# One transposing transfer of a group's split context where there were two

## What is computed

```python
x = _layernorm(x + _L0_attn_ref(x, ...))          # linear attention
x = _layernorm(x + _L0_xattn_ref(x, ctx, ctx, ...))
x = _layernorm(x + _L0_ffn_ref(x, ...))
# inside _L0_xattn_ref:
    attn = jax.nn.softmax(scores, axis=-1)
    ctx = jnp.einsum('bhqk,bhkd->bhqd', attn, V)
    ctx = ctx.transpose(0, 2, 1, 3).reshape(B, S, D)
    out = jnp.einsum('bsd,ed->bse', ctx, Wo) + bo
```

## Time and profile before

| | |
|---|---|
| median of 3 runs | 673.92 us (671.83 to 674.71) |
| profiled execution | 673.73 us, of which the span of the trace is 671.9 us |
| busy, share of the span | PE 96%, PEld 68%, DVE 79%, ACT 66%, POOL 67% |
| mean granted TensorE clock | 0.992 of full speed |
| transfers `cT<-cs` | 30, median 3.4 us from issue to landing |

### The profile page before, as it was taken

The page is one execution under the profiler, slowest core; times in us unless marked ns, Lnnn a source line. Parts: engine busy times, 40 slices in busy tenths (PEclk is TensorE's granted clock), DMA queues, the critical chain, the costliest instruction groups (busy, mean ns, idle before and its releaser), DMA issues.

```text
span 671.9 us, 30473 instructions
## 1 busy us (share of the span) xinstructions
PE 646.1 (96%) x13160; PEld 456.5 (68%) x13160; DVE 532.7 (79%) x1479; ACT 440.6 (66%) x761; POOL 450.5 (67%) x497
## 2 busy tenths in 40 slices
PE   9999999999999999999999999999999999999695
PEld 6766767766766766676676667667677666776474
DVE  1656678788888878898787888878888888777687
ACT  4546465849578584957758494875849487886362
POOL 3234134867769596777959677695977779687552
PEclk9999999999999999999999999999999999999798
DMA  8102122362452434344453536236343634431400
GB/s 335 33 18 34 36 49 53 37 109 52 88 91 50 110 51 100 50 96 83 50 114 49 98 51 114 65 51 112 66 90 50 121 50 69 70 74 35 81 34 33
DMA packets 118905, 49.53 MB, mean 74 GB/s; under 512 B 109425, under 2 KB 109810, under 8 KB 118642
## 3 DMA queue, kind: packets, MB, share of 16 engines
q1 hardware_dynamic: 118770, 47.57, 36.6%
HBM read 16.88 MB, written 4.19 MB: 31 GB/s over the span
## 4 chain that ended last, share of the span: by engine, by line
PE 77%; POOL 9%; DMA 5%; issue 3%; DVE 3%; ACT 2%; SPq 1%; POOLq 0%; DVEq 0%; ACTq 0%
PE bank L330 14%; PE bank L347 8%; PE bank L320 7%; PE bank L400 4%; PE bank L428 4%; PE bank L443 4%; DMA cT<-cs 2%; POOL gall L1104 2%; PE bank L343 2%; PE bank L270 2%; PE bank L287 2%; PE bank L511 2%; PE bank L313 2%; PE bank L272 2%; PE bank L271 2%
## 5 line engine op out<-in xcount | busy, mean ns | idle before, releaser
L330 PEld LDWEIGHTS bank<-Mh,GT 128*32 128x32 f32 x4096 | 110.6, 110 | 25.9 <-issue 20.0
L330 PE MATMUL bank<-Mh,GT 128*32 128x128 f32 x4096 | 126.9, 274 | 1.4 <-issue 1.0
L897 DVE TENSOR_REDUCE mx<-bank 128x8 f32<-128x512 f32 x128 | 78.2, 682 | 13.8 <-PE bank L400 13.6
L1104 POOL TENSOR_TENSOR gall<-gall,lnr 128x512 f32<-128x512 f32 x56 | 71.1, 1281 | 16.8 <-DVE st L867 16.8
L846 DVE COPY GT<-bank 128x512 f32<-128x512 f32 x76 | 49.7, 687 | 35.4 <-PE bank L330 19.9
L662 ACT ACTIVATE PT<-bank 128x512 f32<-128x512 f32 x128 | 64.7, 621 | 10.7 <-PE bank L428 10.7
L1062 POOL TENSOR_TENSOR rstd<-ve,mhalf 128x4 f32<-128x4 f32 x64 | 66.5, 1039 | 5.3
L347 PE MATMUL bank<-Cb,qT 128*64 128x128 f32 x1024 | 66.8, 273 | 0.0
L320 PE MATMUL bank<-kp,xs 64*128 64x512 f32 x256 | 64.3, 617 | 0.0
L1109 POOL TENSOR_TENSOR gs<-gall,gs 128x512 f16<-128x512 f32 x56 | 64.0, 1162 | 0.1
L549 ACT ACTIVATE Mrow<-bank 64x128 f16<-64x128 f32 x16 | 4.3, 271 | 86.3 <-PE bank L409 86.3
(11 more groups left out here) (196 smaller groups left out, 1672.2 us busy)
## 6 DMA issues: line engine op xcount, KB each, us to landing
xT<-in_xT SPq DMA_DIRECT2D x16, 256.0 KB, 3.0
xs<-in_x_nat SPq DMA_DIRECT2D x16, 256.0 KB, 3.8
cxT<-in_cxT SPq DMA_DIRECT2D x16, 256.0 KB, 3.8
out_y<-yo SPq DMA_DIRECT2D x15, 256.0 KB, 2.0
Qm<-in_Wvp SPq DMA_DIRECT2D x1, 1024.0 KB, 7.2
gT<-gs SPq DMA_TRANSPOSE x56, 3.5
gall<-in_Wff SPq DMA_DIRECT2D x1, 768.0 KB, 9.9
small<-in_small SPq DMA_DIRECT2D x1, 523.0 KB, 8.4
```

What stands on the lines that cost most here:

```text
L330: m = e.matmul(bk[32 * j:32 * j + 32, tile(g_)], GT[b % 4][:, tile(hh, 32)], Mh[:, tile(hh)], start=True, stop=True)
L897: e.tensor_reduce(mx[s % 2][:, c0:c0 + 8], bank[uses["score", s, i][0]][:, :].rearrange("p (n k) -> p n k", k=64), AX.X, ALU.max).then_inc ...
L1104: e.tensor_tensor(g[t][:, :], g[t][:, :], lnr[:, :], ALU.mult).then_inc(s_gs, 1)
```

## The change

The two halves' tiles `cs[0]`, `cs[1]` and `cT[0]`, `cT[1]` become halves of one tile each, of 1024 columns. SP issues one transfer for both, at the place of the second one and after the second half's low part; the first half's issue is gone. One semaphore stands for the whole transfer, so `proj0` and `proj1` both wait for it, and so does ACT before it overwrites either half for the next group.

```diff
-        rs, cn, cT = [...], [...], [sb(f"cT{i}", 512, F16) for i in two]
-        cs = [sb(f"cs{i}", 512, F16) for i in two]
+        rs, cn, cT = [...], [...], sb("cT", 1024, F16)
+        cs2, cT2 = sb("cs", 1024, F16), cT
+        cs, cT = [cs2[:, 512 * i:512 * i + 512] for i in two], [cT2[:, 512 * i:512 * i + 512] for i in two]
...
                 else:
                     w.wait_ge(s_xwl, 1)
-                    w.wait_ge(s_cT[tp], 16 * (s + 1))
+                    w.wait_ge(s_cT, 16 * (s + 1))
...
-            def cturn(s, tp):
-                w.wait_ge(s_cl, 2 * s + tp + 1)
-                if s > 0:
-                    w.wait_ge(*filled("proj", s - 1, tp))
-                e.dma_start(cT[tp][:, :].rearrange("p (n c) -> p n c", n=4), cs[tp][:, :], transpose=True).then_inc(s_cT[tp], 16)
+            def cturn(s):
+                w.wait_ge(s_cl, 2 * s + 2)
+                if s > 0:
+                    w.wait_ge(*filled("proj", s - 1, 1))
+                e.dma_start(cT2[:, :].rearrange("p (n c) -> p n c", n=8), cs2[:, :], transpose=True).then_inc(s_cT, 16)
...
-                elif name == "cs":
-                    cturn(s, t)
+                elif name == "cs" and t == 1:
+                    cturn(s)
```

More of the change, by code:

```diff
@@ L147, in decoder_kernel @@
         mx, Mrow, M2 = [sb(f"mx{i}", 64) for i in two], [sb(f"Mrow{i}", 128, F16, 64) for i in two], [sb(f"M2{i}", 1024, F16) for i in two]
-        rs, cn, cT = [sb(f"rs{i}", 32) for i in two], [sb(f"cn{i}", 256) for i in two], [sb(f"cT{i}", 512, F16) for i in two]
-        cs = [sb(f"cs{i}", 512, F16) for i in two]
+        rs, cn, cT = [sb(f"rs{i}", 32) for i in two], [sb(f"cn{i}", 256) for i in two], sb("cT", 1024, F16)
+        cs2, cT2 = sb("cs", 1024, F16), cT
+        cs, cT = [cs2[:, 512 * i:512 * i + 512] for i in two], [cT2[:, 512 * i:512 * i + 512] for i in two]
         x2 = [sb(f"x2{i}", 512) for i in two]
@@ L154, in decoder_kernel @@
         gT = [gTs[:, 1024 * t:1024 * t + 1024] for t in range(4)]
-        gT32, cT32, tpw = [v.bitcast(F32) for v in gT], [v[:, :].bitcast(F32) for v in cT], xT
+        gT32, cT32, tpw = [v.bitcast(F32) for v in gT], [v.bitcast(F32) for v in cT], xT
         st, mv, ve, rstd = [{k: sb(n + k, c) for k in "1234"} for n, c in (("st", 24), ("mv", 8), ("ve", 4), ("rstd", 4))]
@@ L171, in decoder_kernel @@
         s_nr, s_ms, s_x2c = sem("mean_rstd"), sem("mean_part"), sem("x2_less_mean")
-        s_ch, s_cl, s_cT = sem("c_hi"), sem("c_lo"), [sem(f"c{t}_transposed") for t in two]
+        s_ch, s_cl, s_cT = sem("c_hi"), sem("c_lo"), sem("c_transposed")
         s_xwh, s_xwl = sem("xW_hi"), sem("xW_lo")
@@ L671, in chi @@
                 if s > 0:
-                    w.wait_ge(s_cT[tp], 16 * s)
+                    w.wait_ge(s_cT, 16 * s)
                 e.activation(cs[tp][:, 0:256], cn[tp][:, :], ACT.Copy).then_inc(s_ch, 1)
```

## The result

The changed kernel takes 677.3 us (median of 20 runs, 672.39 to 679.22) against 673.93 us for the kernel before (20 runs, 671.01 to 677.03): a ratio of 1.0051, with a 95% interval from 1.0031 to 1.0070, so 3.4 us more. Measured again, beside the last experiments and with runs of the kernel before beside it, it was 680.59 against 675.0 us, 1.0087 (1.0065 to 1.0109), 5.9 us more. I go by these ratios; they are not exactly the quotients of the two medians, and differ from them by up to 0.2%. Both intervals lie above no change. The forecast was 676.4 us.

What follows compares the result with a forecast made beforehand. PE, busy 96% of the span, was taken to set the pace outside the ends. From the profiled 673.73 us, 673.73 - 3.7 + 3.2 + 0.6 + 2.6 = 676.4 us, with an 8 in 10 range of 672.5 to 680.

Steps and rivals of the forecast that it cites:

- The removed waits: Periods, second projection of groups 2, 4 and 7: PE's waits between the two projections can't occur any more, -3.7 us.
- The late transfers in the periods: First projection of the 12 period groups: a bit under half the merged transfers delayed to about 4.2 us, +3.2 us.
- SP's queue: One issue of 1.2 us gone from each group, ahead of the `gT` issues: costed at nothing, bounds 0 and -2 us.
- Group 13: Tail, group 13's first projection: starts later because it waits for the whole transfer, +0.6 us, bounds 0 and 2.
- Group 14: Tail, group 14's first projection: the only transfer is issued at 631.20, PE goes on at 634.4, not 631.82, +2.6 us.
- The slow clock stays: Rival, tail: clock still 1.2 GHz at the last group's probabilities, 2 to 2.5 us more, 678.6 us; chance 0.12.
- Late as a rule: Rival: merged transfers take 4.2 to 4.7 us in most groups and in the tail, 681.8 us; chance 0.09.
- Never late: Rival, periods: the merged transfer is never late, so the 3.2 us go, 673.2 us; chance 0.18.
- hidden by the tail: Rival, tail: something else holds the last group's probabilities, so group 14 costs little, 673.8 us; chance 0.07.
- One fixed cost less per group: Rival: each transfer is paid in full, so dropping 15 gives 638 us; chance 0.02, shared with anything beyond 670.5.

Runs made afterwards that it cites:

- the shifted code: PE's code shifted by some 36 matmuls with smaller fillers at the start: changed kernel 683.2 us, 1.0124; kernel before 677.27 us, 1.0029, both against the kernel before.

## Why the prediction held

The time came out 0.9 us above the forecast and inside the range of 672.5 to 680. The second measurement, 680.59, lies just outside, beside a kernel before that was itself 1 us slower. The mechanism held term by term, with luck in two sizes.

**The removed waits, -3.7 us, held.** The waits between the two projections are gone in every group, and nothing else took their place there.

**The late transfers in the periods, +3.2 us, held in number, and in size with luck.** I took a bit under half of 12 as delayed to about 4.2 us. Six were, by 3.75 to 4.87, mean 4.25; two of these were still covered. The other four cost PE, as the distance between starts less the 0.20 us of an unhindered one, 0.77 + 1.18 + 0.46 + 0.82 = 3.2 us. The net of the two terms, -0.5 us, stands against -0.8 (-2.4 to +0.7) for the kernel that merges only there. By the working's own numbers a late transfer costs 4.2 - 3.1 less a spare of 0.6 to 0.8, that is 0.3 to 0.5 us and not the 0.6 that I put in, so the term should have read 1.6 to 2.7, and its upper bound 5 to 8 and not 12. The measured spare is 0.6 us in each of the four (4.45 - 3.1 - 0.77 in group 5); they were later than I had assumed, 4.5 us in mean, and that made up for it. What I had missed is why a transfer is late: I had it as a chance in each group, where, as far as the sorting shows, it is a packet of code that falls there. It recurs: groups 3, 5, 8, 10 and 12 were late in both profiles of the changed kernel, at 3.75 to 4.97 us.

**SP's queue at nothing: held.** The `gT` waits went from 1.0 to 0.9 us in sum.

**Group 13, +0.6 us, held where its transfer is on time**: 0.7 us in the second profile (1.22 against 0.52). In the first the transfer took 4.42 us and cost 2.2, just above the bound of 2 that I had set. The term left out that this transfer can be late like the others.

**Group 14, +2.6 us, held against the one profile of before**: from the scores to the projection 2.75 and 2.77 us more in the two profiles. PE's idle time there was 4.47 us, and 5.39 in the second, where I had 5.2; what decides is when PE can go on, 3.4 us after the issue, itself 3.1 us after the scores began, as before. The distance to the end stayed at 40 us, as the step said that it would: all of the shift went through. But I took the 631.82 of that profile as the kernel's own time, though the late first half stands in it. Against the 2.14 us seen where it was on time the merge costs 4.35 us here. How often it is late in the kernel before isn't known: it was in the kept trace and, at 4.4 us, in that of the shifted code.

**The tail is undersized by the runs.** The two terms make 3.2 us, the profiles 3.5 to 4.9, the kernel merged in the tail alone 5.0 (3.3 to 6.7). Part of the difference is group 13's late transfer, and part can be the first half of group 14 in the kernel before: where it is on time, the two terms make 5 to 6.5 us. The intervals do not decide between these.

**The rivals.** *The slow clock stays* is refuted by the row it named: the granted clock reads 1.00 from 638 to 641, and the distance to the end did not grow. In the second profile, where the low level holds for about 5 us behind the projection and not 3, it is 40.1 and not 39.8. The Trainium skill, page "TensorE: Matmul & The Clock Gate", section "HAM oscillation — how this bites in real kernels", has the penalty on top of the wait. Here the clock was low behind the wait both before and after the change, and 2.75 us more of waiting added no more than themselves.

*Late as a rule* is refuted: half were. It has a true core, since on the shifted code 8 of 12 were late and the changed kernel took 683.2 us; so the count seems to depend on where code is loaded. *Never late* and *hidden by the tail* are refuted by the rows above. *One fixed cost less per group* is refuted by the kernel that merges in the periods alone: thirteen transfers fewer, and no change that can be told. The half-size transfer takes 2.4 us at least and the whole one 3.1, so some 1.7 us of either do not grow with the size, an estimate from these two; they are spent beside PE's work. The Trainium skill, "DMA: Bandwidth & Descriptors", "Anatomy of one DMA — SWDGE (gpsimd) path", gives a fixed cost of about 2.0 us for a DMA issued from GpSimd. The estimate from the rows, for transfers issued by SP, is near it.

## What to carry to other kernels

Count the waits that a merge removes, not the transfers. Here, with PE 96% busy, thirteen transfers fewer saved nothing that could be told, and the merge cost time where the first half used to be ready long before the second: look for the group with the widest distance between the two halves, and for how much hangs on its first consumer. If the merge is wanted, move the producer of the second half first; here one step moved forward in the order of ACT, POOL and SP took 3.1 us off the 6.5 between group 14's scores and its projection.

## What the hardware showed

A transposing transfer `cT` of 128 x 1024 of 16 bit took 3.1 us in the median when no 16 KB packet of the instruction queue began 0.5 to 2.9 us after its issue, and 3.3 to 5.2 us when one did, in 63 of 67 cases. The four exceptions are packets that began 2.46 to 2.59 us after the issue, with the transfer at 3.1; one at 2.86 us, for group 7 in the first profile, went with a transfer of 4.87, so the moment alone doesn't decide. This rests on where the packets begin in thirteen traces and on one edit, in two kernels, that moved them and, with them, the late transfers; how the two get in each other's way inside the DMA engines was not tried. Its consequence, if the packets are the cause, was a surprise: 36 more matmuls of code at the start, with no more work in them, went with 2 us more in the kernel before (0.1 to 3.8), as much as many changes are worth. Whoever compares two single profiles should look for such packets first: one went with 1.6 us of the kernel before's tail.
